# Modulated convolutions and adapter layers: the whole first phase issued inside the setup block, with the merge of layer 2's adapters between its stages

## What is computed

```python
def _layer(x, style, w, b, mw, mb, typ):
    s = style @ mw.T + mb
    weight = SCALE * w * s[:, None, :, None]
    demod = lax.rsqrt(jnp.sum(weight * weight, axis=(2, 3)) + EPS)
    weight = weight * demod[:, :, None, None]
    ...
# layer 0: x + convs(x) @ (W + sum of adapters).T + bias
# layer 2: the same form; its adapters are chosen by a gate for each group of samples
```

## Time and profile before

| what | value |
|---|---|
| median of 3 runs | 1269.06 us (1266.49 to 1272.35) |
| profiled execution, device time | 1269.14 us |
| its span | 1267.3 us, 1.84 us less |
| PE busy | 1202.5 us, 95% |
| DVE, ACT, POOL busy | 510.3, 355.7, 541.9 us |
| first and second of the page's 40 slices of PE | 4 and 8 tenths, from the third on mostly 8 and 9 |

### The profile page before, as it was taken

The page is one execution under the profiler, slowest core; times in us unless marked ns, Lnnn a source line. Parts: engine busy times, 40 slices in busy tenths (PEclk is TensorE's granted clock), DMA queues, the critical chain, the costliest instruction groups (busy, mean ns, idle before and its releaser), DMA issues.

```text
span 1267.3 us, 46113 instructions
## 1 busy us (share of the span) xinstructions
PE 1202.5 (95%) x21528; PEld 692.8 (55%) x21528; DVE 510.3 (40%) x989; ACT 355.7 (28%) x758; POOL 541.9 (43%) x411
## 2 busy tenths in 40 slices
PE   4868899999999999999999999999999999999997
PEld 3423456555566556555565555565555555665555
DVE  4913233444343344344334344344343333434343
ACT  1322223323322223223222223323222222322321
POOL 2526653345555542455353541655332444634400
PEclk9889999999999999999999999999999999999999
DMA  8053200001421200002101200002101200000101
GB/s 298 35 192 134 102 2 2 2 3 60 162 75 42 95 2 3 2 3 94 69 35 69 102 3 3 2 2 92 71 36 52 86 3 2 2 2 13 58 2 67
DMA packets 20829, 65.82 MB, mean 52 GB/s; under 512 B 4032, under 2 KB 4288, under 8 KB 16160
## 3 DMA queue, kind: packets, MB, share of 16 engines
q1 hardware_dynamic: 18960, 60.85, 13.2%
q10 hardware_dynamic: 1680, 2.04, 0.5%
HBM read 44.00 MB, written 18.87 MB: 50 GB/s over the span
## 4 chain that ended last, share of the span: by engine, by line
PE 87%; DVE 4%; issue 2%; POOL 1%; DMA 0%; ACT 0%; POOLq 0%; DVEq 0%
PE bank_b L1188 27%; PE bank_a L1115 13%; PE bank_b L1099 11%; PE bank_a L1099 11%; PE bank_b L87 8%; PE bank_a L1125 5%; PE bank_a L75 4%; PE bank_b L1146 2%; PE bank_b L1140 2%; PE bank_b L1200 2%; PE bank_b L1181 1%; DVE z L1009 1%; PE bank_b L1159 1%; PE bank_b L1169 1%; PE bank_b L1202 1%
## 5 line engine op out<-in xcount | busy, mean ns | idle before, releaser
L772 POOL TENSOR_TENSOR sum_v<-raw_v 128x768 f32<-128x768 f32 x31 | 57.2, 1846 | 607.0 <-ACT raw_v L830 607.0
L1188 PE MATMUL bank_b<-w_hi,y3t_hi 128*128 128x512 f32 x512 | 208.5, 407 | 1.9 <-issue 1.9
L1188 PE MATMUL bank_b<-w_hi,y3t_lo 128*128 128x512 f32 x512 | 202.8, 396 | 0.0
L1188 PE MATMUL bank_b<-w_lo,y3t_hi 128*128 128x512 f32 x512 | 202.4, 395 | 0.0
L1115 PE MATMUL bank_a<-y,w_down 64*32 64x512 f32 x3072 | 174.0, 596 | 1.7 <-ACT wv L832 1.7
L1099 PE MATMUL bank_b<-y,wv 32*64 32x512 f32 (+2 forms) x3584 | 145.7, 487 | 5.6 <-PEq L195 5.6
L1099 PE MATMUL bank_a<-y,wv 32*64 32x512 f32 (+2 forms) x3584 | 142.8, 480 | 4.8 <-issue 4.8
L959 DVE TENSOR_TENSOR x<-bank_b,x 128x512 f32<-128x512 f32 x96 | 66.4, 692 | 195.5 <-PE bank_b L1188 156.6
L824 ACT ACTIVATE y<-bank_a,cb,tab 128x512 f32<-128x512 f32 x64 | 49.7, 777 | 312.4 <-PE bank_a L1115 312.4
L1188 PEld LDWEIGHTS bank_b<-w_hi,y3t_hi 128*128 128x128 f32 x512 | 96.7, 189 | 36.6 <-issue 15.4
L1115 PEld LDWEIGHTS bank_a<-y,w_down 64*32 64x32 f32 x3072 | 55.3, 107 | 102.8 <-issue 102.8
(11 more groups left out here) (212 smaller groups left out, 1511.0 us busy)
## 6 DMA issues: line engine op xcount, KB each, us to landing
w_hi<-w_scratch SPq DMA_DIRECT2D x9, 1024.0 KB, 5.3
w_lo<-w_scratch SPq DMA_DIRECT2D x9, 1024.0 KB, 8.2
x_in<-in_x SPq DMA_DIRECT2D x32, 256.0 KB, 4.2
out_x<-out_tile SPq DMA_DIRECT2D x32, 256.0 KB, 2.4
w_raw<-w_scratch SPq DMA_DIRECT2D x3, 1024.0 KB, 9.8
w_scratch<-w_hi SPq DMA_DIRECT2D x3, 1024.0 KB, 3.9
...
```

The source lines that it names most:

```text
L772: ins = g_.tensor_tensor(dst[:, :, at:at + count].rearrange("p r k o -> p r (k o)"), src[:, :, 0:count].rearrange("p r k o -> p r (k o)"), ...
L1188: ins = pe.matmul(lin_ps[b][:], y3t[yi][:, k, P * b:P * (b + 1)], w[use(m) % 2][wi][:, k], start=(k == 0 and i == 0), stop=(k == KB - 1 an ...
```

## The change

1. Banks, `y2`, `y3`, `x0`, `w_raw`, `w_sum` and the semaphores of phase 0 are allocated for both blocks. `w0` is merged in place in `w_raw`; its way through DRAM is gone. Several setup tensors now lie over tensors that are free at that time (`a0`, `b0` over `y2[1]`, the parts for `down` over `y3`, `a1`, `b1` over `mod`, `a2eff` over `w_sum`, `b2eff` over `w0_add`).
2. The two table entries that need modulations alone (T_S and T_A + 1, one now with its factor of SCALE) are made right after the modulations and give `scale_ready`. Squares move from DVE to ACT.
3. The rest of phase 0 (`conv2`, its evacuations, `down`), POOL's part of it, and of phase 1 the input, products and blur sums are issued in the setup block. `down` is the last work of PE there.
4. PE's order: the merge of layer 0 comes after `conv0`; the shared adapter of layer 2 stands between `conv2` and `products(1)`, its gated ones between `products(1)` and `down`.
5. SP loads x before the adapters, and `w2`, `b2`, `a2` after `conv0`. Main no longer waits for `a2_out` ahead of its start; SP waits for it inside main. Main's loops begin at n = 1, with `evacuate_3(0)` and `weights_hi(0)` ahead.

```diff
+            sp.wait_ge(square_ready, 1)
+            sp.wait_ge(scale_ready, 1)
+            for name, dst, src in (("a1", a1, io["a1"][:, :, 0:P]), ("b1", b1, io["b1"])):
+                sp.dma_start(dst, src).then_inc(loaded[name], 16)
+            sp.wait_ge(keep["c0_done"], 1)
+            for name, dst, src in (("w2", w2[:], io["w"][:, 2]), ("b2", b2[:], io["b2"]), ("a2", a2[:], io["a2"])):
+                sp.dma_start(dst, src).then_inc(loaded[name], 16)
+            sp.wait_ge(keep["xb_ready"], ROWS)
+            for b in range(ROWS):
+                sp.dma_start(keep["x_in"][:, b], io["x"][1][:, b]).then_inc(keep["x_loaded"][b], 16)
...
+            act.wait_ge(loaded["cw"], 16)
+            for k in range(CONVS):
+                a.activation(sq[:, :, k], cw[:, k], ACT.Square).then_inc(squares, 1)
...
+            products(0)
             for p in range(KB):
+                if p == KB - 1:
+                    act.wait_ge(keep["c0_done"], 1)
+                    act.wait_ge(a_ready, 1)
+                    for r in ON_ACT:
+                        a.activation(y0[:, r, PAD:PAD + LEN], bank_b[r][:], ACT.Identity, bias=column(T_B, r),
+                                     scale=column(T_A, r)).then_inc(keep["y0_act"], 1)
                 act.wait_ge(w0_done, p + 1)
-                a.activation(w0_add[:, p], ps[p][:], ACT.Copy).then_inc(w0_copied, 1)
-            act.wait_ge(keep["pr_done"], 1)
...
+            evacuate_2(1)
+            products(1)
+            act.wait_ge(w0_ready, KB)
...
+            scaled_weights(0)
+            pool.wait_ge(pads_zero, 1)
+            scaled_input(0)
             pool.wait_ge(loaded["coeffs"], 16)
...
+                g.tensor_tensor(x[:, b], keep["x_in"][:, b], keep["ob"][:, 0], ALU.add).then_inc(keep["xb_ready"], 1)
+            scaled_weights(1)
             pool.wait_ge(loaded["w0"], 16)
             for p in range(KB):
                 pool.wait_ge(w0_copied, p + 1)
                 g.tensor_tensor(w0[:, p], w0_add[:, p], w0[:, p], ALU.add).then_inc(w0_ready, 1)
+            pool.wait_ge(keep["c0_done"], 1)
+            scaled_input(1)
+            blurred(1)
 
         @block.vector
         def _(dve):
...
+            S_SIDE = 0
+            v.tensor_copy(table[:, :, :, T_S], m(0, S_SIDE))
+            then(v.tensor_tensor(table[:, :, :, T_A + 1], m(1, S_SIDE), m(2, S_SIDE), ALU.mult))
+            v.tensor_scalar(table[:, :, :, T_A + 1], table[:, :, :, T_A + 1], 0.25 * SCALE, None,
+                            ALU.mult).then_inc(scale_ready, 1)
+            dve.wait_ge(squares, CONVS)
             then(v.tensor_tensor(sq[:, :, :, 0], sq[:, :, :, 0], sq[:, :, :, 1], ALU.add))
...
-            then(v.tensor_scalar(of_a, of_a, SCALE, None, ALU.mult))
-            v.tensor_scalar(table[:, :, :, T_A + 1], table[:, :, :, T_A + 1], 0.25, None, ALU.mult)
-            v.tensor_tensor(table[:, :, :, T_B], bias(0), d(1), ALU.mult)
-            v.tensor_copy(table[:, :, :, T_S], m(0, S_SIDE)).then_inc(scale_ready, 1)
...
+            ins.then_inc(a_ready, 1)
+            dve.wait_ge(a_ready, 1)
 
             dve.wait_ge(keep["c0_done"], 1)
             for r in ON_DVE:
-                v.tensor_scalar(y0[:, r, PAD:PAD + LEN], w2_ps[r][:], column(T_A, r), column(T_B, r),
...
+                ins = v.tensor_scalar(part_dn[:, :, :, i], cw[:, 3], f, None, ALU.mult)
+            then(ins)
+            for n in range(TAPS):
+                blocks_of((n, *DOWN[n]))
+            dve.wait_ge(w0_done, KB)
+            v.memset(y2[1][:, :, 0:HALO:HALO - 1], 0.0)
+            for u in range(2):
+                ins = v.tensor_tensor(add[:, :, u], m_v(1, u), bias(2), ALU.mult)
...
+            for n in range(TAPS, 2 * TAPS):
+                blocks_of((n, *DOWN[n]))
+            evacuate_2(1)
+            dve.wait_ge(loaded["w2"], 16)
+            for p in range(KB):
+                dve.wait_ge(w2_done, p + 1)
+                v.tensor_tensor(w2[:, p], w2_ps[p][:], w2[:, p], ALU.add).then_inc(w2_ready, 1)
...
             pe.wait_ge(up_ready, 1)
             pe.wait_ge(keep["w2s_ready"], 1)
             pe.wait_ge(mod_ready, 3)
-            product_tiles(pe, w2_ps, keep, 0).then_inc(keep["pr_done"], 1)
+            product_tiles(pe, bank_a, keep, 0).then_inc(keep["pr_done"], 1)
+            pe.wait_ge(keep["xs_ready"], ROWS)
+            pe.wait_ge(pads_zero, 1)
+            pe.wait_ge(var_ready, 1)
+            conv0_tiles(pe, bank_b, keep, 0).then_inc(keep["c0_done"], 1)
+            pe.wait_ge(b0_ready, 2)
+            pe.wait_ge(loaded["a0"], 16)
+            pe.wait_ge(keep["raw_ready"], ROWS)
+            pe.wait_ge(keep["ghosts_ready"], ROWS)
+            for p in range(KB):
...
+            pe.wait_ge(w0_copied, 2)
             for l in range(LAYERS):
                 for kind in range(3):
...
-            pe.wait_ge(keep["xs_ready"], ROWS)
-            pe.wait_ge(pads_zero, 1)
-            pe.wait_ge(keep["raw_ready"], ROWS)
-            pe.wait_ge(keep["ghosts_ready"], ROWS)
...
+            pe.wait_ge(keep["y0_act"], 2)
+            pe.wait_ge(keep["y0_dve"], 2)
+            pe.wait_ge(keep["wv_ready"], 1)
+            conv2_tiles(pe, bank_b, keep, 0).then_inc(keep["c2_done"], 1)
+            pe.wait_ge(w0_copied, KB)
+            pe.wait_ge(bias_copied, 2)
+            conv2_tiles(pe, bank_a, keep, 1).then_inc(keep["c2_done"], 1)
+            pe.wait_ge(loaded["as2"], 16)
+            pe.wait_ge(loaded["bs2"], 16)
+            pe.wait_ge(keep["y2_ends"], 1)
+            for p in range(KB):
+                pe.matmul(w2_ps[p][:], as2[:, p * P:(p + 1) * P], bs2[:], start=True, stop=True).then_inc(w2_done, 1)
+            pe.wait_ge(keep["w2s_ready"], 2)
+            pe.wait_ge(keep["y2_ends"], 2)
+            product_tiles(pe, bank_a, keep, 0).then_inc(keep["pr_done"], 1)
 
             pe.wait_ge(gm_ready, 4)
...
-            pe.wait_ge(bias_copied, 2)
             g2 = gmat[:].rearrange("p k b r -> p k (b r)")
-            for banks, raw, done in ((b2_ps, b2, b2_done), (a2_ps, a2, a2_done)):
-                if done is a2_done:
-                    pe.wait_ge(loaded["as2"], 16)
-                    pe.wait_ge(loaded["bs2"], 16)
...
 
+            pe.wait_ge(down_ready, 1)
+            pe.wait_ge(keep["raw_ready"], 2 * ROWS)
+            pe.wait_ge(keep["ghosts_ready"], 2 * ROWS)
+            for u in range(2):
+                down_tiles(pe, bank_a, keep, 0, u).then_inc(keep["dn_done"], 1)
...
-            load_raw(0)
+            for s in keep["a2_out"]:
+                sp.wait_ge(s, 16)
             load_adapters(0)
-            for n in range(PHASES + 1):
+            keep_weights(0, 0)
+            load_raw(1)
+            for n in range(1, PHASES + 1):
...
-                if n and convolve:
+            evacuate_3(0)
+            weights_hi(0)
+            for n in range(1, PHASES + 1):
+                m, convolve = n - 1, n < PHASES
```

More of the change, by code:

```diff
@@ L187, in setup_program @@
     cw = keep["cw"]
-    xs, y0, w2s, raw_v, sum_v, wv = (keep[n] for n in ("xs", "y0", "w2s", "raw_v", "sum_v", "wv"))
     def column(kind, r):
@@ L284, in _ @@
                 a.activation(b2eff[0][:, h], b2_ps[h][:], ACT.Copy).then_inc(b2_hi, 1)
+            for name, raw, hi, *_ in small:
+                act.wait_ge(loaded[name], 16 * (len(PASSES) if name == "b3" else 1))
+                a.activation(hi, raw, ACT.Copy).then_inc(small_hi, 1)
             for h in range(2):
@@ L455, in _, with blocks_of @@
                                 ALU.mult, ALU.add).then_inc(keep["y0_dve"], 1)
+            def blocks_of(terms):
+                out, (t0, f0), *rest = terms
+                out = w_dn[:, :, out]
+                if not rest:
+                    v.tensor_copy(out, part_dn[:, :, t0, f0]).then_inc(blocks, 1)
+                    return
+                (t1, f1), *rest = rest
+                ins = v.tensor_tensor(out, part_dn[:, :, t0, f0], part_dn[:, :, t1, f1], ALU.add)
+                for t2, f2 in rest:
+                    then(ins)
+                    ins = v.tensor_tensor(out, out, part_dn[:, :, t2, f2], ALU.add)
+                ins.then_inc(blocks, 1)
@@ L515, in _ @@
             last.then_inc(var_done, 1)
-            pe.wait_ge(b0_ready, 2)
-            pe.wait_ge(loaded["a0"], 16)
-            pe.wait_ge(var_ready, 1)
-            for p in range(KB):
-                for kk in range(2):
-                    last = pe.matmul(ps[p][:], a0[:, kk, p * P:(p + 1) * P], b0[:, kk], start=(kk == 0), stop=(kk == 1))
-                last.then_inc(w0_done, 1)
             pe.wait_ge(up_ready, 1)
@@ L1037, in adapter_turned @@
                                     ALU.subtract).then_inc(zt_ready, 1)
-            for n in range(PHASES + 1):
-                m, convolve, linear = n - 1, n < PHASES, n > 0
-                if n and convolve:
+            evacuate_3(0)
+            v.memset(logits[:], 0.0)
+            for n in range(1, PHASES + 1):
+                m, convolve = n - 1, n < PHASES
```

(18 more changed lines are left out.)

451 lines of the change are left out of this document (231 added, 220 removed).

## The result

The changed kernel took **1257.18 us** in the median of four runs (1250.18 to 1261.57), the kernel before 1270.7 (1266.49 to 1275.45) beside it: a ratio of 0.9874, 95% interval 0.9829 to 0.992. The profiled execution took 1256.99 us. The forecast of 1253.0, in a range of 1243 to 1261, was right in sign and size; by the medians the gain was 13.5 us where 16.1 were forecast. The start of phase 1's `conv0`, on which it was built, came at 87.60 us (forecast 87.8).

What follows compares the result with a forecast made beforehand. PE holds 87% of the chain, so only its waits or work ahead of phase 1's conv0 count. Setup's steps bring that start from 103.92 to 87.8: 1269.14 - 16.1 = 1253.0 us, range 1243 to 1261.

Steps and rivals of the forecast that it cites:

- t: Start of phase 1's conv0 in the changed kernel: forecast 87.8 us, against 103.92 before; the gain is 103.92 - t.
- Step 6, the tail: PE's end of setup: shared adapter, products, gated adapters at 7.1 and 8.8 us, down 5.3; from 57.7 to 86.7.
- rival C: PE's clock stays low after idling, giving back 10 to 14 of the 16 us: 1263 to 1268; chance 0.07.
- Step 4: PE until conv2: conv0 to 31, merge of layer 0 9.98, biases 2.98, to 44; conv2 begins at 46.1 us.
- the prediction's lower bound of 82: t with POOL not in DVE's way: a_ready 35.6, PE's own work holds conv2 until 44; 78 without stalls, so 1243.
- Step 7, the turn: Turn from setup to main, with PE last and not a store: 1.1 us, reaching 87.8.
- Steps 2, 3 and 5, one for one: DVE's small instructions up to table's end each last as long as POOL's beside them: reciprocal 30.6, a_ready 44.5, table_ready 56.0 us.
- The early scales gain little here: Making table scales early in setup was to gain little, since PE's order and DVE's list meet again at the root.
- Rival A: POOL is held up in turn by DVE's instructions in setup: 5 us on top, 1258 (1256 to 1262); chance 0.20.
- step 3: Newton step and table scales beside busy POOL: a_ready 44.5, conv0's evacuation to 46.1, POOL's list ending at 53.6 us.
- Rival B: DVE gets several instructions through in POOL's gaps: step 3 ends near 39, 1247 (1240 to 1249.5); chance 0.20.
- The remainder: Time from phase 1's conv0 to the end of the span: 1163.4 us before, forecast at 1163 within 2.

Runs made afterwards that it cites:

- pool_after_blocks: Changed kernel with POOL's list behind phase 0's sums held until DVE's blocks are made, all ahead of conv2's first evacuation; 1247.1 us, ratio 0.9806 to before.
- pool_after_a: Changed kernel with POOL waiting for a_ready before gmat and all behind it; 1260.94 us, ratio 0.9905 to the kernel before.
- scales_late: Changed kernel with POOL's b0 and gmat first, and its w2s and xs waiting for a_ready; 1264.34 us, ratio 0.9927 to the kernel before.
- the repeat: The changed kernel itself measured once more, nothing altered; 1257.37 us, ratio 0.9886 to the kernel before.

## Why the prediction was right, and where it was not

- **The level.** t was forecast at 87.8 and came at 87.60. The closeness is luck: three errors cancelled, of 1.3 us (DVE), 2 us the other way (the tail) and 0.7 us (the turn). DVE's list began earlier: sums done at 15.37 (forecast 16.5), the reciprocal at 29.22 (30.6). It kept that lead: `a_ready` 43.46 (44.5), `table_ready` 54.7 (56.0), second half's ends 61.26 (62.6).
- **Step 6, the tail, was mis-sized.** The gated adapters were priced at 7.1 and 8.8 from the earlier trace rows and took 11.0 and 7.0. In the window 60 to 70 us the granted clock was 0.54. A low clock that costs time is rival C's effect, at 2 us instead of 10, but waits are not what it needs: in pool_after_blocks PE was busy for 9.81 of the 10 us from 50 to 60, behind 10.00 of 10, and the granted clock was 0.56 there all the same; the first set of gated adapters took 10.4 us. What brings the clock down there is open.
- **Step 4 was mis-sized behind a wait.** The merge of layer 0 and the biases were priced at 9.98 and 2.98 and took 7.13 and 1.54, so PE waited 5.83 us at `conv2` instead of 2. In the changed kernel this costs nothing, but the prediction's lower bound of 82 (78 without stalls and at the full rate) rests on it: pool_after_blocks begins `conv2` at 39.53, not at 44, and reaches 78.19 with its stalls.
- **Step 7, the turn,** was 1.1 us in the estimate and 0.42 in the profile.
- **Steps 2, 3 and 5, one for one,** carried the sum and held: eleven instructions from the reciprocal to `a_ready` took 14.2 us, forecast 13.9. pool_after_a and pool_after_blocks show it as the cause: 1.28 us against 0.22 for the same instruction. It is a mean of unlike ones: two beside the long sums took 2.29 and 2.86.
- **"The early scales gain little here" was wrong.** scales_late shows 5.9 us. I had followed DVE's side up to the root alone, and not POOL's: without early scales its `w2s`, `xs` and sums stand between the table and PE's products.
- **Rival A was true of its mechanism, not of its price.** Beside DVE, POOL's `gmat` took 3.80 us, alone 2.33 (scales_late); four `xs` 4.68 against 4.03; the third sum 2.81 against 2.35. That is 2.6 us, of which the forecast's rows already held 1.6 (3.72 for `gmat`, 4.12 for `xs`, 2.50 for the sum), and with its earlier start the list still ended at 52.6, where step 3 had 53.6. The reciprocal did not hold up POOL: sums inside and behind it took 1.81 and 2.08, as alone. The Trainium skill, "SBUF — State Buffer", section "SBUF: two separate sides", names as the VectorE instructions that take the lock those with two SBUF inputs and those in a 2-port perf mode. The trace agrees for the additions and products of two tensors that were held up, and in that evacuations from PSUM kept their 0.77 each. The reciprocal has one SBUF input and was not held up; but L520 has one too and was (1.28 us against 0.22), so the number of inputs alone doesn't tell them apart, and no run here shows in which mode either ran.
- **Rival B** fell: four of the eleven slipped through (0.59 to 0.84 us), which the two beside the long sums made up for.
- **The remainder** was to be 1163 within 2, and was 1167.5: by the prediction's own sign that part failed. What was wrong in it is the width, since 2 us is less than one execution differs from the next (the repeat had 1162.6), and the 1163.4 it came from was below what the medians of before leave (1164.9 to 1168.6).

Taken back alone, the early scales cost 5.9 of the 16.3 us and the merges between the stages 7.4. Whether the two add was not tried, nor was what is left, and the stages of the phase moved ahead of main's beginning, tried by itself.
